# Attention scores on TensorE: nine units in the first row stage of a round and seven in the second

## What is computed

```
q = (x @ Wq) split into 16 heads of 64;  k, v likewise from x @ Wkv
s = (q * 64 ** -0.5) @ k.T                       # 1024 x 1024 for each head and batch
gm = max of s over a whole row, without the mask
p = where(key after query, 0, exp(s - gm))
out = (p @ v) / (sum of p over a row + 1e-8);    out @ Wo + bo
```

## Time and profile before

| what | value |
|---|---|
| median of three runs | 1767.13 us (1763.93 to 1769.15) |
| the profiled execution: its time | 1768.99 us |
| its span, first to last instruction | 1767.2 us |
| TensorE busy | 1696.0 us (96%), 13205 matmuls |
| VectorE busy | 1330.8 us (75%) |
| GpSimd busy | 1313.0 us (74%) |
| ScalarE busy | 1066.5 us (60%) |
| mean granted TensorE clock | 0.989 of full speed |

### The profile page before, as it was taken

One profiled execution on the slowest core, in us unless ns is written; L12 is line 12 of the kernel. 1 busy time (PEld: TensorE's weight loads), 2 busy tenths in 40 slices (PEclk: granted clock), 3 DMA queues, 4 the chain that ended last, 5 costly groups with the idle time before them and its releaser, 6 DMA issues. The chain is left out here.

```text
span 1767.2 us, 35587 instructions
## 1 busy us (share of the span) xinstructions
PE 1696.0 (96%) x13205; PEld 1226.9 (69%) x13205; DVE 1330.8 (75%) x2397; ACT 1066.5 (60%) x2239; POOL 1313.0 (74%) x1354
## 2 busy tenths in 40 slices
PE   6999999999999999999999999997999878899998
PEld 4767676676767767677676776765788755568886
DVE  7777667676776776777677776755999858989887
ACT  2555545455555555546555465554899877658876
POOL 1677777677786777867767677786899957748998
PEclk9999999999999999999999999998999989999999
DMA  3000000000000000000000000010000000000000
GB/s 97 2 1 1 1 1 2 1 1 2 1 1 2 1 1 1 2 1 1 1 1 2 1 1 1 2 49 9 1 1 1 1 1 1 1 1 7 13 13 19
DMA packets 15149, 11.08 MB, mean 6 GB/s; under 512 B 481, under 2 KB 14594, under 8 KB 14978
## 3 DMA queue, kind: packets, MB, share of 16 engines
q1 hardware_dynamic: 14978, 8.80, 1.8%
HBM read 6.70 MB, written 2.10 MB: 5 GB/s over the span
## 5 line engine op out<-in xcount | busy, mean ns | idle before, releaser
L1207 DVE TENSOR_REDUCE attn_neg<-attn_shared 128x2 f32<-128x1024 f32 x512 | 611.9, 1223 | 236.3 <-PE attn_shared L1390 234.9
L1052 ACT ACTIVATE attn_prob<-attn_shared 128x1024 f32<-128x1024 f32 x288 | 295.4, 1027 | 360.6 <-PE attn_shared L1417 360.4
L948 POOL TENSOR_TENSOR attn_row_sum<-attn_row_sum,attn_prob 128x1024 f32<-128x1024 f32 (+3 forms) x256 | 418.7, 1636 | 24.5 <-POOL attn_row_sum L948 0.4
L312 ACT ACTIVATE experts_weighed<-experts_y,kept_gate 128x128 f32<-128x128 f32 x1024 | 279.7, 413 | 47.7 <-PE experts_y L559 40.0
L925 POOL TENSOR_TENSOR attn_prob<-attn_prob,attn_below 128x256 f32<-128x256 f32 x256 | 190.2, 743 | 158.1 <-ACT attn_prob L1052 158.0
L405 DVE SCALAR_TENSOR_TENSOR experts_acc<-experts_y,kept_gate,experts_acc 128x128 f32<-128x128 f32 x896 | 247.6, 346 | 22.4 <-PE experts_y L559 20.2
L1386 PE MATMUL attn_shared<-attn_qk_hi 64*128 64x512 f32 x1024 | 228.3, 429 | 8.2 <-DVE attn_neg L1207 2.3
L557 PE MATMUL experts_y<-kept_w_hi,kept_xT_hi 128*128 128x512 f32 x512 | 205.0, 400 | 4.8 <-PEq L726 1.8
L943 POOL TENSOR_TENSOR attn_row_sum<-attn_prob 128x1024 f32<-128x1024 f32 x64 | 135.8, 2122 | 97.6 <-ACT attn_prob L1052 95.1
L558 PE MATMUL experts_y<-kept_w_lo,kept_xT_hi 128*128 128x512 f32 x512 | 200.8, 392 | 0.0
L559 PE MATMUL experts_y<-kept_w_hi,kept_xT_lo 128*128 128x512 f32 x512 | 200.5, 392 | 0.0
(11 more groups left out here) (283 smaller groups left out, 3597.2 us busy)
## 6 DMA issues: line engine op xcount, KB each, us to landing
kept_x<-in_L_attn_a_x_dram SPq DMA_DIRECT2D x4, 512.0 KB, 8.5
kept_half_raw<-_ffn_expert_weights_dram SPq DMA_DIRECT2D x4, 512.0 KB, 4.8
out_dram<-kept_x SPq DMA_DIRECT2D x8, 256.0 KB, 2.3
attn_prob<-in_L_attn_a_Wkv_dram SPq DMA_DIRECT2D x2, 512.0 KB, 6.0
attn_prob<-in_L_attn_a_Wq_dram SPq DMA_DIRECT2D x1, 512.0 KB, 4.9
attn_wo<-in_L_attn_a_Wo_dram SPq DMA_DIRECT2D x4, 128.0 KB, 5.2
attn_bo<-in_L_attn_a_bo_dram SPq DMA_DIRECT2D x1, 64.0 KB, 6.4
linear_weights_raw<-in_L_attn_b_Wg_dram SPq DMA_DIRECT2D x1, 64.0 KB
```

The lines of the kernel that those rows point to most:

```text
L312: ins = act.activation(weighed[n][:, e, :], y[fill(pair, quad, odd) % RING][:, e * D:(e + 1) * D], ACT.Copy, scale=k.gate[:, c, quad * PER ...
L948: pool.tensor_tensor(row_sums(p, n)[:, :, at:], row_sums(p, n)[:, :, at:], src, ALU.add).then_inc(add_ok, 1)
L1052: act.activation(prob[n % RING][:, :, :], buffer((p, t))[:, :, :], ACT.Exp).then_inc(exp_ok, 1)
L1207: dve.tensor_reduce(neg[p % 2][:, :, b, half], buffer((p, b, half))[:, :, :], AX.X, ALU.max, negate=True).then_inc(max_ok, 1)
```

## The change

```diff
-    STAGES = ("stststststsss", "stsstsstssts")
+    STAGES = ("stststststssss", "ststststsss")
+    FIRST_SCORES = 9
...
     def score_units(p, t):
 
-        return [(p, b, half) for b in S_BLOCKS[4 * t:4 * t + 4] for half in (1, 0)] if valid(p) else []
+        units = [(p, b, half) for b in S_BLOCKS for half in (1, 0)] if valid(p) else []
+        return units[FIRST_SCORES:] if t else units[:FIRST_SCORES]
```

## The result

| what | before | with the change |
|---|---|---|
| median, runs taken side by side | 1766.58 us (4 runs) | 1756.18 us (4 runs, 1755.96 to 1758.96) |
| ratio, with its 95% interval | | 0.9949 (0.9937 to 0.9960) |
| span of the profiled execution | 1767.2 us | 1754.2 us |

The change makes the kernel 0.5% faster, 9.0 us by the ratio (7.1 to 11.1). The forecast was 8.7 us less and 1758.4 us.

What follows compares the result with a forecast made beforehand. TensorE bounds the kernel, with some 0.7 us of waiting or late weight loading in each stage 1. 0.88 - 1.16 = -0.28 us a round, -8.7 us over 31 rounds, gives 1758.4 us against 1767.13; range 1751 to 1768.

Steps and rivals of the forecast that it cites:

- What bounds: TensorE, 96% busy; only its waits can go, some 0.7 us of each stage 1, 22 us over 31 rounds.
- Stage 0, one more unit: End of stage 0: a fourth score unit in the tail waits for its buffer and costs 0.88 us.
- Stage 1: One score unit fewer and a new order: 9.11 us in place of 10.27, a gain of 1.16 us.
- three fits of 0.03 to 0.05 us: New stage 1: buffers for score units, the last score unit and the first projection come free just in time.
- The third fit, at the projection: End of stage 1: the projection's buffer is free at 9.06 us, the projection comes at 9.11; fits by 0.05.
- the slower rival: End of stage 1: projection waits up to 1.13 us longer for its buffer, +1.08 a round, 1792 us; chance 0.06.
- VectorE's queue: Ninth maximum delays reciprocals and statistics 1.13 us; slack 1.2 us before stage 1, 0.7 before low parts: cost 0.
- Round -1 and the rest: Round -1 with 9 and 7 units, round 31 without score units, ScalarE, GpSimd and transfers: all cost 0.
- Sum: 0.88 - 1.16 = -0.28 us a round, -8.7 us over 31 rounds, forecast median 1758.4 us.
- nothing left: Rival: the fits in stage 1 fail, weights load late, its gain shrinks to 0.88 us; 1767 us, chance 0.14.
- all waiting gone: Rival: added unit costs 0.75 us, stage 1 loses 1.35, -0.6 a round; 1749 us, chance 0.09.
- The clock: Rival: TensorE's clock falls to the 1.2 GHz level over four units, 2.8 us a round; 1844 us, chance 0.01.

Runs made afterwards that it cites:

- short maxima: Kernel before and changed kernel, each maximum reading 256 of the 512 columns: 1744.7 us with the old order, 1746.1 us with the new one.
- with four: Against the kernel before: eight score units in each stage, stage 1 reordered to ststststssss, four score units ahead of the projection; 1762.5 us, ratio 0.9975.
- the split alone: Against the change: nine and seven score units kept, stage 1 in the order of before less its last unit; 1773.7 us, ratio 1.0041 to the kernel before.

## Why the prediction was right

- *What bounds*: that TensorE's busy row hides the waits was right. By it 0.15 us of stage 1 could be won; 0.34 us of a single wait went, and some 0.17 us of late weight loads and smaller waits. The stage went from 10.27 to 9.05 us, of which 0.70 are the unit that left it.
- *Stage 0, one more unit*: forecast 0.88 us, measured 0.91 (11.615 - 10.707, the means with one place more). The unit was to start 2.28 us after the first of the tail and starts 2.27 after it. The last two units took 0.85 and 0.89 us in the mean of the rounds, in place of the 0.85 and 0.87 forecast: 0.02 of the 0.03. The rest is too small for rows of two places.
- *Stage 1*: forecast 9.11 us and a gain of 1.16, measured 9.05 and 1.21. The three fits of 0.03 to 0.05 us held: with short maxima, where nothing has to fit, the same stage takes 9.04. The last unit takes 0.83 us (648.34 to 649.17), not the 0.88 taken from the last unit of the old stage, which itself stood behind a tile of 384 and 128. That is the 0.05.
- *The third fit, at the projection*: it held, but not as it was worked out, and with some luck. The first maximum of the tail starts 7.75 us into the stage (647.87 - 640.12; 7.73 in the mean of the rounds), not the 7.68 forecast, since behind a tile of 384 and 128 a maximum starts 0.96 us after its unit (646.91) and not 0.90. By the prediction's own words a delay of over 0.05 us was to decide for the slower rival. What made up for it was the turning of the maxima: the projection comes 0.09 us behind the end of the stage, 9.14 us into it, and this was not in the 9.11. It starts 0.18 us after the maximum that it needs has ended (mean of the rounds), of which 0.15 are the handover, so the slack is 0.03 us.
- *VectorE's queue*: the reciprocals and statistics were forecast to end 1.13 us later and cost nothing, with a slack of 1.2 us ahead of stage 1 in this round; 1.35 us was left. Ahead of the low parts 0.7 us was forecast and 0.41 measured; `smallest`, left out of that sum, takes 0.17 of the difference. The low parts wait for ScalarE either way, so both costs are 0.
- *Round -1 and the rest*: forecast 0. The first turned matmul starts at 46.9 us in place of 47.0, so 0.
- *Sum*: -0.28 us a round forecast, -0.30 measured; -8.7 us against -9.4 in the stages and -9.0 by the ratio of the runs. Cost and gain were both too small, by 0.03 and 0.05 us, and these errors partly cancel. The median lies 2.2 us below the forecast of 1758.4; 0.7 of them are the stages, and the rest is no more than the scatter behind the attention.
- *Rivals*: nothing left, all waiting gone: the measured round lies between, near the forecast. The wait at the projection did not come with three units ahead of it. It does exist: with four, it is 0.15 us a round, and takes a part of the gain. The clock: granted 1.00 in the new stage 1 and in the attention from 46 to 1160 us, as the windows show:

```profile
core 0: us, PE busy (x) PEld busy (x) DVE busy (x) ACT busy (x) POOL busy (x), PEclk, DMA share, GB/s
640.10:649.20 9.10, 9.10 (x95) 7.40 (x91) 6.24 (x6) 4.11 (x4) 7.10 (x12) 1.00 0.00 1
46.00:1160.00 1114.00, 1113.38 (x10406) 771.25 (x10410) 807.95 (x754) 600.47 (x869) 828.28 (x816) 1.00 0.01 2
```

One thing the prediction did not ask: whether the split was needed. It priced both parts nearly right, and from its own numbers (0.88 for the unit in stage 0, 0.70 to 0.88 for the one that leaves stage 1) it could have said that the split gives nothing and the order everything. The run of the split alone shows it: 0.90 us paid, 0.74 won.

The weight loads' share, which the Trainium skill names as the better yardstick (Perfetto Trace Analysis, "Identifying the Most-Contended Engine"), is 7.40 of 9.10 us here, 81%, and was 8.20 of 10.30, 80%. As a measure of the waiting that can be won this trace does not bear it out: by it 1.7 us of the new stage are unused, and with short maxima the stage is only 0.01 us shorter. It rises by under two points where half a microsecond of waiting and late loading goes. The lengths from start to start told the two stages apart.

## What to carry to other kernels

Where an engine that works in order fills a small ring of buffers, and two other engines read them, count the starts, not the busy time. A unit that reuses a buffer should start no sooner after the one before it in that buffer than three times together: until the reader starts, the reader's own time, and the handover. Here these are 0.90 + 1.23 + 0.15 = 2.28 us for a score unit. Put units of the slow reader and of the quick one in turns, and put what is over in a tail with work behind it that needs no buffer. In this kernel a tail one unit longer than the ring of three cost about 0.2 us more than the unit itself, and the fifth unit cost the reader's whole pace of 1.13 us. Before moving work between stages, price the order alone.

## What the runs showed of the hardware

- Reductions of 128 x 1024 values from PSUM take 1.23 us each by their rows, but follow each other at 1.13 us where they queue (four in 4.62 us, (4.62 - 1.23) / 3). Half as many columns take 0.69 us, not half of 1.23.
- A buffer handed back by VectorE lets a matmul that waits for it start 0.15 to 0.17 us after the reduction's end, by the rows of the runs with whole maxima.
- A unit whose release comes just in time is still 0.03 to 0.08 us longer than one that never waited (before, round 16: 634.78 to 635.51 is 0.73 us and 651.42 to 652.20 is 0.78, against 0.70). Its weights load late: from 634.71 on, 0.07 us ahead of its first matmul, where those of the unit at 634.08 load from 633.85 on, 0.23 us ahead.
